# Values and their sums from one product per head, in an attention kernel on one Trainium2 core

## What is computed

```
att = einsum('bhtd,bhsd->bhts', q, k) / sqrt(D)
att = where(mask == 0, -inf, att)          # causal, and every 4th key is left out
y = einsum('bhts,bhsd->bhtd', softmax(att), v)
return y.transpose(0, 2, 1, 3).reshape(B, T, C) @ Wp + bp
```

## Time and profile before

| | us |
|---|---|
| median of 3 runs | 857.08 (855.34 to 858.67) |
| the profiled execution, its own time | 859.55 |
| its span, first to last instruction | 857.7 |
| PE busy over the span | 744.2 (87%) |
| DVE busy over the span | 573.1 (67%) |
| ACT busy | 397.3 (46%) |
| POOL busy | 374.7 (44%) |

### The profile page before, as it was taken

One profiled execution on the slowest core, in us unless ns is written; L12 is line 12 of the kernel. 1 busy time (PEld: TensorE's weight loads), 2 busy tenths in 40 slices (PEclk: granted clock), 3 DMA queues, 4 the chain that ended last, 5 costly groups with the idle time before them and its releaser, 6 DMA issues. The chain is left out here.

```text
span 857.7 us, 18735 instructions
## 1 busy us (share of the span) xinstructions
PE 744.2 (87%) x6840; PEld 673.3 (78%) x6840; DVE 573.1 (67%) x1343; ACT 397.3 (46%) x857; POOL 374.7 (44%) x504
## 2 busy tenths in 40 slices
PE   3699999999999999999997511379999999999994
PEld 2577888888888888888885411369999999999994
DVE  1135777668768768667664378776787787887561
ACT  0214455454455455455443155035557366475570
POOL 3113464464465454465444223023537347355334
PEclk9899999999999999999998755569999999999998
DMA  8952675555774675475661342011344453442122
GB/s 273 307 96 48 89 117 97 86 104 98 108 119 99 94 99 96 103 119 99 96 90 51 94 149 74 29 28 43 72 132 64 117 144 49 127 102 32 34 32 32
DMA packets 80686, 82.36 MB, mean 96 GB/s; under 512 B 36161, under 2 KB 74943, under 8 KB 80244
## 3 DMA queue, kind: packets, MB, share of 16 engines
q1 hardware_dynamic: 67980, 66.92, 38.8%
q0 software_dynamic: 11584, 10.96, 8.2%
q10 hardware_dynamic: 1032, 3.30, 1.1%
HBM read 34.59 MB, written 16.22 MB: 59 GB/s over the span
## 5 line engine op out<-in xcount | busy, mean ns | idle before, releaser
L595 POOL DMA_INDIRECT out<-r_arena x48 | 80.3, 1674 | 118.2 <-DVE r_arena L1530 107.9
L656 ACT ACTIVATE r_arena<-ps_all 126x660 f32<-126x660 f32 x128 | 92.2, 720 | 56.9 <-PE ps_all L879 55.3
L1249 DVE RECIPROCAL r_arena<-ps_all 128x165 f32<-128x165 f32 x64 | 76.1, 1189 | 61.3 <-PE ps_all L894 61.3
L520 POOL TENSOR_SCALAR_AFFINE_SELECT r_arena<-r_arena 126x660 f32<-126x660 f32 x128 | 97.0, 767 | 45.9 <-ACT r_arena L656 45.5
L1238 DVE TENSOR_REDUCE mx<-ps_all 128x4 f32<-128x504 f32 (+1 forms) x160 | 105.0, 669 | 15.3 <-PE ps_all L856 13.8
L879 PE MATMUL ps_all<-Qp,Kp 98*126 98x166 f32 x512 | 84.6, 289 | 7.9 <-ACT r_arena L656 6.1
L856 PE MATMUL ps_all<-Kp,Qp 96*65 96x56 f32 (+1 forms) x512 | 90.6, 293 | 0.0
L1552 DVE TENSOR_TENSOR hT_lo<-r_arena,hT_hi 128x330 fp32r<-128x330 f32 x128 | 63.2, 502 | 39.8 <-ACT r_arena L760 39.6
L582 POOL DMA_INDIRECT xe<-xn_rows,r_arena x48 | 59.8, 1245 | 63.4 <-issue 36.5
L1111 PE MATMUL ps_all<-xeT_hi,W_hi 128*128 128x330 f32 x256 | 83.1, 325 | 1.1 <-DVE hT_lo L1552 1.1
L758 ACT ACTIVATE hT_hi<-ps_all,vec_s 128x330 fp32r<-128x330 f32 x128 | 68.9, 539 | 32.4 <-PE ps_all L1111 30.1
(11 more groups left out here) (178 smaller groups left out, 1706.6 us busy)
## 6 DMA issues: line engine op xcount, KB each, us to landing
H<-w SPq DMA_DIRECT2D x16, 1024.0 KB, 5.6
Qp<-q_hi SPq DMA_DIRECT2D x64, 166.0 KB, 3.9
Kp<-k_hi SPq DMA_DIRECT2D x128, 63.0 KB, 4.1
Qp<-q_lo SPq DMA_DIRECT2D x32, 166.0 KB, 4.7
out<-H SPq DMA_DIRECT2D x16, 330.0 KB
xn_rows<-r_arena SPq DMA_DIRECT2D x16, 330.0 KB
Kp<-k_lo SPq DMA_DIRECT2D x64, 63.0 KB, 4.1
H<-h SPq DMA_DIRECT2D x1, 3360.0 KB, 22.6
```

What stands on the lines that cost most here:

```text
L520: pool.affine_select(PT[0:S, g, :, :], PT[0:S, g, :, :], [[0, 4], [STEP - 1, T]], ALU.is_ge, 0.0, base=STEP - 2, channel_multiplier=-STEP) ...
L595: pool.indirect_dma_start(rows_out, bass.IndirectOffsetOnAxis(tok[0:A, e % NTB, a:a + 1], 0), yw[0:A, a, :], None, bounds_check=NTOK - 1, ...
L656: act.activation(PT[0:S, g, :, :].rearrange("p (k h) t -> p k h t", k=2), pair[:, :, :, 0:T], ACT.Exp, scale=float(HD) ** -0.5).then_inc(e ...
L1249: dve.reciprocal(rS[:, c, :], bank(2 + c)[:, T:2 * T]).then_inc(rs_sum, 1)
```

## The change

The values get a column of ones beside each of their columns: `V` is now `[head, 16, 2]`, with 1.0 in every second place, so that one product per head leaves value and sum on neighbouring partitions (even: value, odd: the same sum). The separate product with `ones_eo` goes. The two heads of a strip no longer add into one region but lie side by side in the bank, 165 columns each. ACT copies each half of the heads out of PSUM (`copy_heads`: 128 x 330), DVE takes the reciprocal of all of that copy (`invert`), and after both halves two DMAs of SP (`move_heads`) bring the second head's values to the odd partitions and the first head's inverses to the even ones. The product (`heads_out`) has moved to the next round, between `row_max(2)` and `row_max(3)`, and reads two SBUF tiles instead of PSUM and SBUF. `Wp` and the bias of v are permuted outside to fit. `Kp`'s order of dimensions changes, so that a pack DMA writes a contiguous stretch per partition.

```diff
-        ones_eo = kf("ones_eo").rearrange("p (w n) -> p w n", w=2)
...
-        R_ARENA = sb("r_arena", [128, 8576])
+        R_ARENA = sb("r_arena", [128, 8906])
...
-        rS = cut(R_ARENA, KD, T)
+        y_raw = cut(R_ARENA, 2, KD, T)
...
-            Qp, Kp = sb1("Qp", [128, 3, HC, TE], F32R), sb1("Kp", [128, 3, HC, 2, S], F32R)
+            Qp, Kp = sb1("Qp", [128, 3, HC, TE], F32R), sb1("Kp", [128, 3, 2, HC, S], F32R)
...
-            V = sb1("V", [128, 3, 2, 272])
+            V = sb1("V", [128, 3, NH, HD, 2])
+            y_inv = sb1("y_inv", [128, 2, KD, T])
...
-                        sp.dma_start(Kp[32 * row + HD * w:32 * row + HD * w + HD, i, :, w, :].bitcast(F32),
+                        sp.dma_start(Kp[32 * row + HD * w:32 * row + HD * w + HD, i, w].bitcast(F32),
                                      src[64 * w:64 * w + 64, h, :, :].bitcast(F32)).then_inc(qk_packed[i], 16)
+
+            def move_heads(b):
+                sp.wait_ge(y_inverse, 2 * b + 2)
+                sp.dma_start(y_raw[1:128:2, 0], y_raw[0:128:2, 1]).then_inc(y_moved, 16)
+                sp.dma_start(y_inv[0:128:2, 1], y_inv[1:128:2, 0]).then_inc(y_moved, 16)
...
                     pack_max(b + 1)
+                if 0 <= b < B:
+                    move_heads(b)
                 if u == 1 and 0 <= n - 1 < NPAIR:
                     store_h(n - 1)
...
-                    zero(V[:, :, :, :])
+                    pool.memset(V[:, :, :, :, :], 1.0).then_inc(pinit_done, 1)
...
+            def copy_heads(b, c):
+                act.wait_ge(pv_done, 2 * b + c + 1)
+                if b >= 1:
+                    act.wait_ge(yT_ready, 2 * b + c - 1)
+                act.activation(y_raw[:, :, c, :], bank(2 + c)[:, 0:2 * T].rearrange("p (w t) -> p w t", w=2), ACT.Copy)\
+                   .then_inc(y_copied, 1)
...
                 if u == 1 and 0 <= n - 1 < NPAIR:
                     copy_xn2T(n - 1)
+                if 0 <= b < B:
+                    copy_heads(b, 0)
+                    copy_heads(b, 1)
...
                 if b >= 1:
-                    pe.wait_ge(yT_ready, 2 * b + c - 1)
+                    pe.wait_ge(y_copied, 2 * b + c - 1)
                 for w in range(2):
-                    for part in range(2):
-                        for j in range(4):
-                            dst = bank(2 + c)[32 * j:32 * j + 32, part * T:(part + 1) * T]
-                            lhs = v_rows(b % 3, w, 4 * c + j)[0:S] if part == 0 else ones_eo[0:S, w, :]
-                            mm = pe.matmul(dst, lhs, PT[0:S, 2 * c + w, j, :], start=(w == 0 and part == 0),
-                                           stop=(w == 1), skip_group_check=True)
+                    for j in range(4):
+                        mm = pe.matmul(bank(2 + c)[32 * j:32 * j + 32, w * T:(w + 1) * T],
+                                       V[0:S, b % 3, 2 * (4 * c + j) + w].rearrange("p d o -> p (d o)"), PT[0:S, 2 * c + w, j, :], start=(w == 0),
+                                       stop=(w == 1), skip_group_check=True)
                 mm.then_inc(pv_done, 1)
...
+            def invert(b, c):
+                dve.wait_ge(y_copied, 2 * b + c + 1)
+                dve.reciprocal(y_inv[:, :, c, :], y_raw[:, :, c, :]).then_inc(y_inverse, 1)
+
             def heads_out(b, c):
                 n, u = divmod(b, 2)
-                dve.wait_ge(pv_done, 2 * b + c + 1)
-                dve.reciprocal(rS[:, c, :], bank(2 + c)[:, T:2 * T]).then_inc(rs_sum, 1)
-                dve.wait_ge(rs_sum, 2 * b + c + 1)
+                dve.wait_ge(y_moved, 32 * b + 32)
                 if n >= 2 and c == 0 and u == 0:
                     dve.wait_ge(proj_done, RT * (n - 2) + RT)
-                dve.tensor_tensor(yT[:, n % 2, c, u * T:(u + 1) * T], bank(2 + c)[:, 0:T], rS[:, c, :], ALU.mult)\
+                dve.tensor_tensor(yT[:, n % 2, c, u * T:(u + 1) * T], y_raw[:, 0, c, :], y_inv[:, 1, c, :], ALU.mult)\
                    .then_inc(yT_ready, 1)
...
                 if has_r:
                     row_max(b + 1, 2)
+                for c in range(KD):
+                    if 1 <= b <= B:
+                        heads_out(b - 1, c)
                 if has_r:
                     row_max(b + 1, 3)
...
                 if has_s:
-                    heads_out(b, 0)
-                    heads_out(b, 1)
+                    invert(b, 0)
+                    invert(b, 1)
                 if u == 1 and has_p:
                     copy_logits(n - 1)
```

More of the change, by code:

```diff
@@ L73, in _columns @@
     f32["ident"] = np.eye(128)
[L74 to L77, removed]
     p = np.arange(128)
@@ L197, in build @@
         yT = cut(R_ARENA, 2, KD, PAIR)
-        rS = cut(R_ARENA, KD, T)
+        y_raw = cut(R_ARENA, 2, KD, T)
+        xn2T = cut(R_ARENA, KD, PAIR)
         xc = cut(R_ARENA, RT, D)
         xn2 = cut(R_ARENA, 2, RT, D)
-        xn2T = cut(R_ARENA, KD, PAIR)
         at[0] = 0
@@ L219, in build @@
         SGN = cut(R_ARENA, ONACT, SEGT)
-        at[0] = 4 * 4 * T + 2 * KD * PAIR + KD * T + 3 * RT * D + KD * PAIR
+        at[0] = 4 * 4 * T + 2 * KD * PAIR + 2 * KD * T + 3 * RT * D + KD * PAIR
         VAL = cut(R_ARENA, NCOL, NV + 1, dt=BF16)
@@ L239, in build @@
             cls_s = sb1("cls_s", [NPAIR, 2, D])
-            Qp, Kp = sb1("Qp", [128, 3, HC, TE], F32R), sb1("Kp", [128, 3, HC, 2, S], F32R)
+            Qp, Kp = sb1("Qp", [128, 3, HC, TE], F32R), sb1("Kp", [128, 3, 2, HC, S], F32R)
             q_hi, q_lo = sb1("q_hi", [128, 2, KD, TE], F32R), sb1("q_lo", [128, 2, KD, TE], F32R)
             k_hi, k_lo = sb1("k_hi", [128, 2, KD, S], F32R), sb1("k_lo", [128, 2, KD, S], F32R)
-            minus_s = sb1("minus_s", [2, HC, 2, S])
+            minus_s = sb1("minus_s", [2, 2, HC, S])
             mT = sb1("mT", [128, 2, TE], F32R)
@@ L265, in bank @@
             return ps_all[:, i, :]
-        def v_rows(i, w, j):
-            return V[:, i].rearrange("p w x -> p (w x)")[:, w * 272 - 16 * w + j * 32:w * 272 - 16 * w + j * 32 + 32]
         x_in = [sem(f"x_in{i}") for i in range(3)]
@@ L288, in build @@
             "q_hi_ready", "k_hi_ready", "rows_done", "max_ready", "mt_done", "mT_ready")]
-        st_done, exp_done, causal_done, pv_done, rs_sum, yT_ready, proj_done, resid_ready = [sem(n) for n in (
-            "st_done", "exp_done", "causal_done", "pv_done", "rs_sum", "yT_ready", "proj_done", "resid_ready")]
+        st_done, exp_done, causal_done, pv_done, y_copied, y_inverse, yT_ready, proj_done, resid_ready = [sem(n) for n in (
+            "st_done", "exp_done", "causal_done", "pv_done", "y_copied", "y_inverse", "yT_ready", "proj_done", "resid_ready")]
         t2_done, xn2T_ready, logit_done, logit_ready = [sem(n) for n in (
@@ L293, in build @@
         h_stored = sem("h_stored")
+        y_moved = sem("y_moved")
         qk_packed = [sem(f"qk_packed{i}") for i in range(3)]
@@ L646, in copy_v @@
                     act.wait_ge(pv_done, 2 * n - 4)
-                act.activation(V[0:S, n % 3, :, 0:D].rearrange("p w (j x) -> p w j x", x=32)[:, :, :, 0:HD],
-                               bank(6)[0:S, 0:D].rearrange("p (j w d) -> p w j d", w=2, d=HD), ACT.Copy)\
+                act.activation(V[0:S, n % 3, :, :, 0], bank(6)[0:S, 0:D].rearrange("p (h d) -> p h d", d=HD), ACT.Copy)\
                    .then_inc(v_ready, 1)
+            def copy_heads(b, c):
[4 more added lines that the diff above has]
+                   .then_inc(y_copied, 1)
             def exps(b, g):
@@ L856, in row_scores @@
                     mm = pe.matmul(dst[0:rows, 2 * j * cols:2 * (j + 1) * cols].rearrange("p (w s) -> p w s", w=2),
-                                   Qp[0:MROW, q, h, at_row:at_row + rows], Kp[0:MROW, q, h, :, 0:cols],
+                                   Qp[0:MROW, q, h, at_row:at_row + rows], Kp[0:MROW, q, :, h, 0:cols],
                                    start=False, stop=(j == len(pairs) - 1), skip_group_check=True)
@@ L878, in key_scores @@
                         h = 4 * (g // 2) + 2 * k + j
-                        mm = pe.matmul(dst[0:S, j * TE:(j + 1) * TE], Kp[0:MROW + 2, q, h, g % 2, :],
+                        mm = pe.matmul(dst[0:S, j * TE:(j + 1) * TE], Kp[0:MROW + 2, q, g % 2, h, :],
                                        Qp[0:MROW + 2, q, h, :], start=(j == 0), stop=(j == 1), skip_group_check=True)
@@ L1625 @@
     perm = np.arange(D).reshape(HC // 2, KD, 2, HD).transpose(1, 2, 3, 0).reshape(D)
-    minus = np.zeros((2, HC, 2, S), f4)
+    mixed = np.arange(D).reshape(HC, 2, HD).transpose(0, 2, 1).reshape(D)
+    minus = np.zeros((2, 2, HC, S), f4)
     for w in range(2):
-        minus[w, :, w] = -1.0
+        minus[w, w] = -1.0
     x = a["x"].reshape(B, CH, IMG // PATCH, PATCH, IMG // PATCH, PATCH)
@@ L1647 @@
         "minus": minus,
-        "watt": np.stack([rows(attn("Wq")[:, perm]), rows(attn("Wk")[:, perm]), rows(attn("Wv")), rows(attn("Wp"))],
```

(3 more changed lines are left out.)

## The result

The changed kernel takes 944.86 us (median of 4 runs, 943.02 to 949.41), the kernel before 857.27 on the same chip: a ratio of 1.103, interval 1.099 to 1.108. The prediction was 938, range 895 to 962. The profiled execution took 943.02 us with a span of 941.2, so its rows can be set against the median as they are.

What follows compares the result with a forecast made beforehand. DVE's loop from values through head work and maxima to the next values was taken as the bound. Intervals 32.3 + 45.0 + 1.4 and tail 4.9, less 2.5, gave 81 on 857: 938 us, range 895 to 962.

Steps and rivals of the forecast that it cites:

- The bound: Attention-stage loop of values, DVE's head work, maxima, max_transposes, values: longer DVE work lengthens the round; PE waits about 2 us.
- the signs that were named: Expected in the profile: reciprocals 2.2 us, little DVE idle before them, DVE share 75 to 80%, PE below 80%.
- The reciprocal: DVE's inverse of 330 columns: 2.22 us, not 1.19, priced by element; by-instruction rival: 839 us, chance 0.04.
- The loop's first leg: From a round's first values (M) to the next first maximum: M + 7.12 after even rounds, M + 7.35 after odd.
- Without blocking: DVE's loop alone, products not held up by POOL: max_transposes late by 1.4 and 1.63 us, total 909.
- Blocking: heads_out's products with two SBUF operands wait for POOL: max_transposes late by 2.15 us in even, 3.0 in odd rounds.
- The rival of no blocking: Alternative outcome: DVE's products and POOL's operations miss each other, 909 us; chance 0.18.
- The intervals: Time between first values of successive rounds: 15.7 us odd to even, 15.0 even to odd, from 13.5 and 12.0.
- The clock: Rival: PE at half clock from max_transposes to the values, 2.4 us more in half the rounds, 975 us; chance 0.17.
- PE's saving: Sums' matmuls dropped: 1.12 us a round, 36 in all; POOL's fourth group gates the values' second half, leaving 20.
- Transfers: move_heads' two 84 KB DMAs land 2.1 to 4.1 us after issue; no wait taken, far end 0.5 a round.
- Tail: After the last round's values: 10.8 us to the last product in place of 5.9, plus 4.9 (3.9 to 5.9).

Runs made afterwards that it cites:

- e4: Changed kernel with heads_out's product replaced by a one-operand reduction of the same 165 columns, nothing normalised: 904.0 us, ratio 1.054.
- e6: Changed kernel with idle matmuls on PE ahead of row_scores(2), 8 in odd rounds and 4 in even ones: 939.9 us, ratio 1.095.
- e1: Kernel before, with the separate sums' product run for the first batch only: 847.9 us, ratio 0.989.
- e7: Changed kernel reworked: two DMAs gather values and sums, then DVE inverts 165 columns; inverse, product and projections later, maxima packed before patches move: 872.3 us, ratio 1.017.
- e10: e7 with key_scores(2) moved ahead of row_scores(4) on PE: 891.7 us, ratio 1.039.
- e2: Kernel before, with each reciprocal taking all 330 columns in place of 165, the extra inverses unused: 941.1 us, ratio 1.098.
- e5: Changed kernel with reciprocals on one head of each strip and the product replaced by a one-operand reduction: 849.8 us, ratio 0.991.
- e9: Kernel before, with key_scores(2) moved ahead of row_scores(4) on PE: 860.3 us, ratio 1.002.

## Why the prediction was right, and where its terms were off

**The bound was read rightly.** Values, head work, maxima, `max_transposes`, values: PE waits for the first maximum about 2 us, as said, in the odd rounds; in the even ones the wait for the copy of the logits (0.83 us at 280.90) stands ahead of it. Two of the signs that were named did not come: PE's share fell to 86.5%, not below 80, since it works longer at half clock; and DVE's idle time before the reciprocals stayed at 57.2 us (61.3 before), since the loop runs over PE between `max_transposes` and the values.

**The reciprocal: right.** 2.187 us against 2.22; by element, not by instruction. By the estimate from the figure of the Trainium skill (VectorE: DVE Perf Modes, "First, the fixed hardware budget") it would have been 2.9; the trace sides with the row. The loop's first leg came out shorter than worked out: the first maximum starts at M + 6.79 in the odd round (259.52 to 266.31; predicted 7.12) and at M + 6.88 in the next even one (275.21 to 282.09; predicted 7.35), because two reciprocals in a row take 4.29 us, and the even round's copy was ready by 0.2 us sooner.

**Without blocking: the total was near, its parts too high.** 909 was worked out for the changed kernel without the block, and e4 took 904. Its common intervals, 13.23 and 14.35 us, are 1.24 and 0.82 above before's 11.99 and 13.53; the prediction had 1.63 and 1.4.

**Blocking: seen, and under-sized.** The prediction gave it 29 us, e4 shows 40.9. At full clock the intervals grow against e4's by 1.35 us in the even round (predicted 0.75) and by 0.88 in the odd (1.37), which makes 33 us in 15 pairs. The other 7 or so go with the clock: from the first to the last values it was at half for 96 us in the changed kernel and for 46 in e4. That the clock makes this rest is argued, not shown. In the even round not one but nearly all of POOL's train is shared: 2.33 us for two products in place of 0.57. The rival of no blocking is refuted by e4.

**The intervals were right in sum.** Odd to even 15.68 was predicted, 15.70 is the common value and 15.86 the mean. Even to odd 15.0 was predicted against a mean of 14.80 (14.98 without the first, which is a short one), but this mean hides several cases, from 14.11 at full clock to 15.7 with a long fall. With the clock held, 2.1 us more than before would have been the right term, not 3.0 (14.11 was seen once in the changed kernel, and 14.11 or 14.12 four times in e6); the clock made up for it.

**The clock: part of the loss, and no rival of its own.** That case gave half of the rounds 2.4 us each, 36 us in all. Falls of 6.3 us or more came in six even-to-odd intervals and cost 1.6 us each (15.69 against 14.11), those of 3.4 us in four and cost 0.25. With the two longest odd-to-even intervals (17.75 and 17.14 against 15.70, both with more than 6 us at half clock) I estimate the clock's share at 14 us. Much of PE's half-clock work lies in DVE's shadow, as was argued against that rival.

**PE's saving: over-sized.** 20 us were said to be left after POOL's gate; e1 shows 10. The step that was mis-sized is what is "left" behind the gate: in e1 PEld waits for POOL 31 times, in every round and not only in the odd ones, and the packed maxima (`key_scores(0)`) make a second gate. It did not enter the sum, since DVE's loop sets the intervals.

**Transfers: right.** 1.9 us from issue to landing for 82.5 KB, and two waits in the stage.

**Tail: 4.9 predicted, 5.3 measured**, though made differently: to the last product 9.2 us (548.78 to 557.99) in place of 10.8 predicted and 5.9 before, 3.3 more; and 2.0 more behind it, where the projections start after 5.4 us of waiting and run at half clock.

**What cancelled.** With the intervals at full clock a pair grows by 2.17 + 2.12 = 4.29 us, where 5.15 was predicted: 13 us less in 15 pairs. The longer intervals, nearly all with a fallen clock, put about 15 us back (14 x (14.98 - 14.11) and 15 x (15.86 - 15.70)). The sum had no term for them, so the hit within 0.7% is partly luck: the mechanism was right, its blocking in the odd round was over-sized, and the clock, which was left to a rival, filled the place. That the fallen clock made these intervals longer is argued from their lengths, which go with the time at half clock, and from PE's rows in one round.

## What to carry to other kernels

Work that is taken from the busiest engine is worth only what the next gate leaves: here 36 us of PE gave 10, since POOL's select and the packed maxima came due right behind it. Before values and their sums are merged into one product, count what the consumer now has to touch: inverting twice the columns cost more than the sums' products had, and the place for the inverse is after the heads have been gathered (e7, 73 us better, with the products and the projections moved too). A DVE operation that reads two SBUF tiles should not stand beside POOL's trains. With one operand in PSUM it can: the product of the kernel before never met a POOL operation, but e7 has such pairs, where `k_lo` reads one tile in SBUF and one in PSUM:

```profile
248.21 0.60 DVE L1225 SCALAR_TENSOR_TENSOR k_lo<-ps_all,vec_s,k_hi 128x126 fp32r<-128x126 f32 x2
...
248.52 2.10 POOL L476 TENSOR_TENSOR H<-H,bpe 110x256 f32<-110x256 f32 x3
```

28 of them overlap a POOL operation on two tiles and take 339 to 344 ns, the others in the stage 337 to 344; POOL's three take 2.10 us as ever.

## What the hardware showed that was not expected

The clock fell after a gap of PE that looked harmless, 1.95 us in a stretch that was otherwise full. The half clock came 1.2 us after PE had taken up work again and lasted 6.8 us. After the same gap in the next odd round it came about 0.5 us after PE's return and lasted 3.4. The same twelve projections took 2.84 us at full clock, 4.53 at a mean of 0.62 (e10) and 5.23 at 0.53 (e7). Keeping PE busy through one gap took 40 of 96 us at half clock away and gave 5 us (e6).

The block is mostly one way. All 51 of DVE's products that met one of POOL's operations on two tiles took 0.85 us or more; the other 13 have a median of 0.33. This is the exclusive port of the Trainium skill (SBUF — State Buffer, "SBUF: two separate sides"), and the trace agrees. POOL lost less. Its three sums took 2.19 us beside the products in place of 2.10. Its three products took 2.27 in place of 1.84, but in the last round, where DVE stood idle, they took 2.09:

```profile
545.34 2.09 POOL L503 TENSOR_TENSOR r_arena<-r_arena,row_s 110x256 f32<-110x256 f32 x3
```

So meeting DVE costs each of them 0.08 us (0.81 against 0.72). The rest, 0.72 against 0.64, has nothing to do with DVE's products: it is there without any meeting, in e2, e4 and e5 as well, and not in e1, e7, e9 and e10. Its cause is open.
